# Centring the rows once, at the end of layer 2, and re-ordering ScalarE, VectorE and GpSimd around it

## The reference, cut to what matters

```
def _layernorm(x, axis=-1, eps=1e-05):
    m = jnp.mean(x, axis=axis, keepdims=True)
    v = jnp.var(x, axis=axis, keepdims=True)
    return (x - m) / jnp.sqrt(v + eps)
...
x = _layernorm(x + _L0_gnn_ref(x, adj, ...), axis=-1)   # attention, softmax over rows
x = _layernorm(x + _L1_gnn_ref(x, adj, ...), axis=-1)   # attention, softmax over columns, elu
x = _layernorm(x + _L2_gnn_ref(x, adj, ...), axis=-1)   # attention, softmax over rows, elu
x = _layernorm(x + _L3_gnn_ref(x, ..., adj, weight, bias), axis=-1)
# layer 3, with a 0/1 adjacency only relation 1 has edges:
#   y = (adj @ x) @ weight[0] + bias
```

## Time and profile before

| what | value |
|---|---|
| time, median of 3 runs | 412.65 us (412.54 to 412.78) |
| the profiled execution, its own time | 413.85 us |
| the profiled execution, its span (first to last instruction) | 411.7 us |
| busy share of the span: PE, PEld, DVE, ACT, POOL | 87%, 77%, 86%, 75%, 74% |
| TensorE clock granted, mean | 0.985 |
| 280 to 300 us (layer 2), busy of 20 us: PE, DVE, ACT, POOL | 19.45, 18.38, 15.24, 15.11 |
| 370 to 380 us (layer 3), busy of 10 us: PE, DVE, ACT, POOL | 9.86, 9.38, 8.23, 9.33 |
| 0 to 60 us | the only stretch in which the DMA engines are busy (0.84 and more of their time) |

### The profile page before, as it was taken

The page is one execution under the profiler, slowest core; times in us unless marked ns, Lnnn a source line. Parts: engine busy times, 40 slices in busy tenths (PEclk is TensorE's granted clock), DMA queues, the critical chain, the costliest instruction groups (busy, mean ns, idle before and its releaser), DMA issues. The chain is left out here.

```text
span 411.7 us, 9207 instructions
## 1 busy us (share of the span) xinstructions
PE 358.6 (87%) x2786; PEld 316.4 (77%) x2793; DVE 355.4 (86%) x1350; ACT 308.9 (75%) x840; POOL 304.9 (74%) x395
## 2 busy tenths in 40 slices
PE   7898999999977888887878889999999779999970
PEld 7697999999977877786878888989898665455550
DVE  0458899999999899999999987999899997899984
ACT  2757999999886776868878786878778647888862
POOL 5356889778788776886757757777777846999994
PEclk9999999999998999999999999999999999999995
DMA  6999973000000000000000000000000000022223
GB/s 164 219 249 247 264 113 53 2 1 2 2 1 2 1 2 0 2 2 0 2 1 2 2 0 2 3 0 2 2 1 2 2 1 0 2 78 78 76 77 108
DMA packets 8757, 18.20 MB, mean 44 GB/s; under 512 B 1281, under 2 KB 2561, under 8 KB 8705
## 3 DMA queue, kind: packets, MB, share of 16 engines
q0 software_dynamic: 2304, 8.39, 10.6%
q1 hardware_dynamic: 5280, 8.72, 6.3%
q10 hardware_dynamic: 1120, 0.46, 0.4%
HBM read 21.76 MB, written 4.19 MB: 63 GB/s over the span
## 5 line engine op out<-in xcount | busy, mean ns | idle before, releaser
L561 PE MATMUL o_ps<-h_scaled,PT 128*128 128x129 f32 (+1 forms) x1536 | 182.4, 277 | 10.3 <-POOL h_scaled L278 6.4
L561 PEld LDWEIGHTS o_ps<-h_scaled,PT 128*128 128x128 f32 x1536 | 176.7, 193 | 13.1 <-issue 9.6
L1043 DVE SCALAR_TENSOR_TENSOR PT<-rows_ps,factors,MT 128x512 f32<-128x512 f32 x128 | 88.7, 736 | 0.0
L805 ACT ACTIVATE X<-y,rstd 128x128 f32<-128x128 f32 x192 | 61.0, 390 | 25.0 <-POOL rstd L319 24.9
L319 POOL TENSOR_TENSOR rstd<-var_eps,neg_half 128x4 f32<-128x4 f32 x64 | 70.3, 1098 | 5.0
L498 PE MATMUL h_ps<-wx,xT 128*128 128x130 f32 x384 | 53.7, 283 | 14.0 <-DVE smax L1004 12.3
L498 PEld LDWEIGHTS h_ps<-wx,xT 128*128 128x128 f32 x384 | 48.5, 194 | 19.7 <-issue 19.5
L1119 DVE BATCH_NORM_STATS2 stats<-y 128x6 f32<-128x128 f32 x256 | 55.6, 280 | 5.8 <-DVE y L1113 0.9
L254 POOL TENSOR_TENSOR mean_term<-h_mean,empty_row 128x512 f32<-128x512 f32 x32 | 38.2, 1194 | 18.7 <-DVE residual L1099 14.1
L334 POOL TENSOR_TENSOR elu_exp<-elu_exp,X 128x512 f32<-128x512 f32 x32 | 40.8, 1275 | 6.7 <-ACT elu_exp L798 6.4
L278 POOL TENSOR_TENSOR h_scaled<-hx,factors 128x516 f32<-128x516 f32 x32 | 35.1, 1097 | 13.5 <-PE o_ps L561 8.2
(11 more groups left out here) (120 smaller groups left out, 660.0 us busy)
## 6 DMA issues: line engine op xcount, KB each, us to landing
MT<-adj_by_j POOLq DMA_DIRECT2D x16, 512.0 KB, 12.9
X<-x SPq DMA_DIRECT2D x16, 256.0 KB, 7.9
out<-X SPq DMA_DIRECT2D x16, 256.0 KB, 2.0
w_rel<-w SPq DMA_DIRECT2D x1, 256.0 KB, 3.5
w_back<-w_by_output ACTq DMA_DIRECT2D x1, 192.0 KB, 3.4
wx<-w_by_input ACTq DMA_DIRECT2D x1, 192.0 KB, 3.8
bias<-b ACTq DMA_DIRECT2D x1, 64.0 KB, 3.0
bias<-b SPq DMA_DIRECT2D x1, 64.0 KB, 5.5
```

Source lines behind the costliest of these rows:

```text
L561: last = pe.matmul(o_ps[it.b][:, ic, first:1 + D], PT[:, it.b, jc, ic * P:(ic + 1) * P], h_scaled[:, it.b, jc, first:1 + D], start=(jc == ...
L805: last = act.activation(X[:, it.g, c, :], y[:, it.b, c, :], ACT.Copy, scale=rstd[:, it.b, c:c + 1])
L1043: dve.scalar_tensor_tensor(out=PT[:, it.b, c, :], in0=rows_ps[:], scalar=factors[:, it.b, 1, c:c + 1], in1=m, op0=ALU.max, op1=ALU.mult, * ...
```

## The change

Rows now leave layer 2 centred. In layer 2 POOL runs `find_offset` and ACT `take_norm`; in layer 3 POOL no longer runs `find_offset`, and both ACT and DVE normalise by `y` times `rstd` alone. For that the first relation's weights and the layer's bias are centred over the output features by four small ACT operations in slots 38 to 41 (`CENTRE_LATE_SLOT` + 0 to 3), in place of PE's product and ACT's copy in slots 46 and 47. In layer 2 ACT copies `hx` and `xT` ahead of the normalisation; in layer 3 it normalises ahead of copying the sums. While item n+1 is of layer 2, DVE's `own_max` stands between the two pairs of `weights` instead of behind them.

```diff
--- before.py
+++ after.py
@@ -26,7 +26,7 @@
 
 LAST_ATTENTION, ATTENTION_END = G * LAYERS - 4, G * LAYERS + 3
 FLAG_SLOT = G * LAYERS + 6
-CENTRE_SLOT, CENTRE_LATE_SLOT = -3, G * LAYERS - 2
+CENTRE_SLOT, CENTRE_LATE_SLOT = -3, G * 2 + 6
 R_EIGHTY, EXPONENT, BIAS, Z, RZ, ABOVE, BELOW, HINGE, WEIGHT = range(9)
 LOWEST, BIG = -430.0, 3e38
 WARM_UP = 12
@@ -130,6 +130,9 @@
         rank_one = sb("rank_one", [P, P], BF16)
         bias2_col = sb("bias2_col", [P, 1])
         bias3 = sb("bias3", [P, D])
+        bias3_in = sb("bias3_in", [P, D])
+        late_scaled = sb("late_scaled", [P, D])
+        late_mean = sb("late_mean", [P, 2])
         ab2_sb = sb("ab2_sb", [P, 2])
         shift_k = sb("shift_k", [P, 5])
         b2_a = sb("b2_a", [P, 2])
@@ -202,7 +205,7 @@
                     sp.wait_ge(sem(f"mask_in{n - 4}"), 16)
                 load_x(item(n))
             sp.dma_start(w_rel[:, :, :], w3.rearrange("r d o -> d r o")).then_inc(sem("w_late"), 16)
-            sp.dma_start(bias3[:, :], b3.partition_broadcast(P)).then_inc(sem("w_late"), 16)
+            sp.dma_start(bias3_in[:, :], b3.partition_broadcast(P)).then_inc(sem("w_late"), 16)
 
             for n in range(G * LAYERS, G * (LAYERS + 1)):
                 it = item(n)
@@ -376,6 +379,8 @@
                     elu_low(at(-1))
                 if at(-2):
                     find_rstd(at(-2))
+                if at(-2) and at(-2).l == 2:
+                    find_offset(at(-2))
                 split_bias2(n)
                 if at(2) and at(2).l == 1:
                     column_weight(at(2))
@@ -388,13 +393,13 @@
 
                     pool.wait_ge(sem("y_sum"), it.done - 2)
                     pool.wait_ge(sem("x_new"), it.done - G)
+                    if it.g == 0:
+                        pool.wait_ge(sem("centred"), 3)
                     pool.tensor_tensor(residual[:, it.b, :, :], X[:, it.g, :, :],
                                        bias3[:, :].unsqueeze(1).broadcast_to([P, C, D]),
                                        ALU.add).then_inc(sem("residual"), 1)
                 if at(-1):
                     find_rstd(at(-1))
-                    if at(-1).g < FIRST_ON_VECTOR:
-                        find_offset(at(-1))
 
             def redo():
                 with pool.Fori(0, G) as g:
@@ -595,10 +600,6 @@
                     pe.wait_ge(sem("centre"), 1)
                     pe.matmul(rows_ps[:, 0:260], centre[:], wx[:, 1:3, :].rearrange("p l w -> p (l w)"),
                               start=True, stop=True).then_inc(sem("centred_ps"), 1)
-                if n == CENTRE_LATE_SLOT:
-                    pe.wait_ge(sem("hx"), G * LAYERS)
-                    pe.matmul(h_ps[:, 1, 0:D], centre[:], w_rel[:, 0, :], start=True, stop=True)\
-                        .then_inc(sem("centred_ps"), 1)
 
             def gather(it):
 
@@ -802,7 +803,7 @@
 
                 act.wait_ge(sem("rstd"), it.done)
                 for c in range(C):
-                    last = act.activation(X[:, it.g, c, :], y[:, it.b, c, :], ACT.Copy, scale=rstd[:, it.b, c:c + 1])
+                    last = act.activation(X[:, it.g, c, :], y[:, it.t, c, :], ACT.Copy, scale=rstd[:, it.t, c:c + 1])
                 last.then_inc(sem("x_new"), 1)
 
             def take_norm(it):
@@ -818,10 +819,16 @@
                     act.wait_ge(sem("centred_ps"), 1)
                     act.copy(wx[:, 1:3, :].rearrange("p l w -> p (l w)"), rows_ps[:, 0:260])\
                         .then_inc(sem("centred"), 1)
-                if n == CENTRE_LATE_SLOT + 1:
-                    act.wait_ge(sem("centred_ps"), 2)
-                    act.copy(w_rel[:, 0, :], h_ps[:, 1, 0:D])\
-                        .then_inc(sem("centred"), 1)
+                late = ((w_rel[:, 0, :], w_rel[:, 0, :]), (bias3_in[:, :], bias3[:, :]))
+                for k, (rows, to) in enumerate(late):
+                    if n == CENTRE_LATE_SLOT + 2 * k:
+                        act.wait_ge(sem("w_late"), 32)
+                        act.activation(late_scaled[:, :], rows, ACT.Copy, scale=-1.0 / D,
+                                       accum_out=late_mean[:, k:k + 1]).then_inc(sem("late_mean"), 1)
+                    if n == CENTRE_LATE_SLOT + 2 * k + 1:
+                        act.wait_ge(sem("late_mean"), k + 1)
+                        act.activation(to, rows, ACT.Identity, bias=late_mean[:, k:k + 1])\
+                            .then_inc(sem("centred"), 1)
 
             def flag(it):
 
@@ -861,19 +868,21 @@
                     node_factors(at(2))
                 if at(-1) and at(-1).l == 2:
                     elu(at(-1))
-                near_column_layer = any(at(k) and at(k).l == 1 for k in (1, -2))
-                if near_column_layer:
+                past_first_layer = any(at(k) and at(k).l >= 1 for k in (1, -2))
+                if past_first_layer:
                     take_next(at)
                 take_bias2(n)
                 if at(2) and at(2).l == 1:
                     above_max(at(2))
-                if at(-3) and at(-3).l != 1:
+                if at(-3) and at(-3).l == 0:
                     take_scaled(at(-3))
+                if at(-3) and at(-3).l == 2:
+                    take_norm(at(-3))
                 if at(-2) and at(-2).l == 1:
                     take_scaled(at(-2))
                 if at(1) and at(1).l == 1:
                     fill_empty(at(1))
-                if not near_column_layer:
+                if not past_first_layer:
                     take_next(at)
                 take_centred(n)
                 if at(2) and at(2).l == 1:
@@ -896,6 +905,8 @@
 
                         act.wait_ge(sem("sums"), it.of_layer - 4)
                     act.copy(split[:, it.r, 0, :, :], X[:, it.g, :, :]).then_inc(sem("split_hi"), 1)
+                if at(-3) and at(-3).g < FIRST_ON_VECTOR:
+                    take_scaled(at(-3))
                 if at(1):
                     it = at(1)
                     act.wait_ge(sem("sums"), it.of_layer)
@@ -903,8 +914,6 @@
 
                         act.wait_ge(sem("att"), it.done - 2)
                     act.copy(xT[:, it.b, :], sums_ps[it.b][:]).then_inc(sem("sum_taken"), 1)
-                if at(-3) and at(-3).g < FIRST_ON_VECTOR:
-                    take_norm(at(-3))
 
             def redo():
                 with act.Fori(0, G) as g:
@@ -1138,10 +1147,8 @@
             def normalize_last(it):
 
                 dve.wait_ge(sem("rstd"), it.done)
-                dve.wait_ge(sem("mean_var"), it.done)
                 for c in range(C):
-                    last = dve.tensor_scalar(X[:, it.g, c, :], y[:, it.t, c, :], mean_var[:, it.t, c, 0:1],
-                                             rstd[:, it.t, c:c + 1], ALU.subtract, ALU.mult)
+                    last = dve.tensor_scalar(X[:, it.g, c, :], y[:, it.t, c, :], rstd[:, it.t, c:c + 1], None, ALU.mult)
                 last.then_inc(sem("x_last"), 1)
 
             def attention_slot(at, n):
@@ -1169,9 +1176,12 @@
                     weights(at(1), (0, 1))
                 if at(-2) and at(-2).l != 1:
                     aggregate(at(-2))
+                early_max = at(1) and at(1).l == 2
+                if at(3) and early_max:
+                    own_max(at(3))
                 if at(1):
                     weights(at(1), (2, 3))
-                if at(3) and not (at(1) and at(1).l == 1):
+                if at(3) and not early_max and not (at(1) and at(1).l == 1):
                     own_max(at(3))
                 if at(3) and at(1) and at(1).l == 1:
                     take_max(at(3))
```

## The result

| | median | spread | runs |
|---|---|---|---|
| before, beside the change | 412.63 us | 412.54 to 412.78 | 4 |
| the change | 406.51 us | 405.24 to 407.46 | 4 |

The profiled execution of the change took 405.65 us for a span of 403.5, so against the profiled execution of before it gained 8.2 us.

What follows compares the result with a forecast made beforehand. It took a ring of two DVE/PE waits to bound layer 2 and POOL layer 3 and the end. Terms -2.8 + 0.5 + 1.1 - 2.05 - 1.9 = -5.15 us off 412.65 gave 407.5 us, 8-in-10 range 405.7 to 410.3.

Steps and rivals of the forecast that it cites:

- layer 2, own_max: Layer 2: early own_max removes DVE's wait for PE, period 6.54 to 6.26 us over ten items, -2.8 us.
- slots 32 and 33: Start of layer 2: DVE stands 1.4 us for hx, later idles take 0.9, leaving +0.5 us (bounds 0 and 1.4).
- ACT's operand, late operations, POOL's offset in layer 2: Layer 2: ACT's +0.37 us an item, four late operations and POOL's 0.49 us offset stay hidden, cost 0.
- hand-over: Slots 47 to 50: ACT's longer normalisations and wait for offset delay DVE's splits, +1.1 us (bounds 0.5 and 2.0).
- layer 3, ten items: Layer 3, steady: without POOL's offset PE paces at 3.48 us an item, -2.05 us over ten items.
- end, to the last normalisation: End: the last y starts 1.65 us sooner after PE's project_sum, plus 0.25 on item 62's normalisation, -1.9 us.
- behind the last normalisation: After the last normalisation: the output transfer stays, no gain.
- such a wait: Layer 2, every slot: own_max waits for hx, slower than before, 415.3 us at 0.5 an item; 6%.
- POOL's margin in layer 2: Layer 2: h_scaled still ends 0.12 us before DVE's y; if it overran, y would stand 0.3 us an item.
- POOL was to show gaps: Sign in layer 3: POOL, needing 3.27 us an item against PE's 3.48, would show gaps in the profile.
- POOL's backlog: End: the last y waited for ACT's normalisation, which waited for POOL's offset; the change leaves POOL no backlog.
- ACT's order: Layer 3: ACT's copy of the sums behind the normalisation, some 1.2 us later, needed only a gather later, cost 0.

Runs made afterwards that it cites:

- the last two experiments: Kernel before with layer 2's two re-orderings alone, 409.43 us; kernel before with ACT's layer 3 normalisation ahead of the sums' copy alone, 412.51 us.
- the other chip: The changed kernel timed once more with no edit, beside the kernel before: 405.58 us, ratio 0.9837.

## Why the prediction was right, and where it was not

| step | predicted | profiled execution | shown by |
|---|---|---|---|
| layers 0 and 1 | 0 | -1.3 | spread, not the change |
| layer 2, own_max | -2.8 | -2.9 | own_max late +2.85 by its trace, re-orderings alone -2.9 |
| slots 32 and 33 | +0.5 | +0.2 | 6.40 against 6.22 |
| ACT's operand, late operations, POOL's offset in layer 2 | 0 | 0 | 6.26 with and without them |
| hand-over | +1.1 | +0.8 | idles 1.46, 1.47, 0.82, 0.22 against 1.27, 1.11, 0, 0.67; 38.58 with ACT's normalisation behind the casts |
| layer 3, ten items | -2.05 | -1.9 | 34.92 in both kernels without offset |
| end, to the last normalisation | -1.9 | -2.1 | two causes, -1.1 and -1.0 |
| behind the last normalisation | 0 | -0.9 | 3.7 against 4.6 |

The rows add to -8.1, of a measured -8.2. How the hand-over's row comes about: take_max of slot 45 stands at 317.79, 4.1 us earlier than in the trace of before (321.90), and project_sum of item 52 at 357.25, 3.3 earlier. Timeline of DVE, the kernel before:

```profile
321.90 0.28 DVE L1004 TENSOR_REDUCE smax<-h_ps 128x1 f32<-128x128 f32 x1
...
341.49 0.69 DVE L1199 TENSOR_TENSOR split<-rest,split 128x512 bf16<-128x512 f32 x1 [1.27 <-ACT split L891]
...
347.45 0.71 DVE L1199 TENSOR_TENSOR split<-rest,split 128x512 bf16<-128x512 f32 x1 [1.11 <-ACT split L891]
```

**Layer 2.** The mechanism held in every part: PE's 6.26 is what is left, and the copy of hx ahead of the normalisation is what makes it possible. Without it the same own_max costs more than it gave. I had given such a wait 6%, and the experiment says how it looks: 0.33 us a slot. The stall in slots 32 and 33 was mis-sized: the wait itself came as worked out (1.33 us, "1.4"), but only 0.2 us of it were left behind DVE's later idles of 0.53 and 0.39, not 0.4 to 0.5; what took up the rest the rows don't show. The second wait, 0.64, cost nothing (248.59 - 242.35 = 6.24 us, with DVE's 0.38 of waiting for PE still in it).

**POOL's margin in layer 2.** I worked out 0.12 us between h_scaled and y. h_scaled ends at 256.25 and y starts at 256.36, 0.11 later, with its full 0.68; with the re-orderings alone, where this margin isn't used, the period is the same 6.26.

**The hand-over** came at +0.8 of +1.1, and by the cause I gave: with the normalisations behind the casts it takes 38.58 us, as in the kernel before (38.62). The place was one slot off: DVE's wait in slot 50, which I had grow from 0.67, shrank to 0.22, and one of 0.82 came in slot 49, where there had been none. Part of ACT's wait for the offset there is POOL's: `offset` took 0.46 us (345.40) instead of 0.20. What I did not see, and expected otherwise when I moved the normalisations (2.3 us), is that the waits which the kernel before has as well do not go with that edit: they come back as longer splits beside POOL's operations. Whether less or later work on POOL would get them back was not tried.

**Layer 3** went as worked out, but for one sign: POOL was to show gaps, and showed none between 357 and 392 us. var_eps and rstd keep their stretched 0.6 and 1.34 us while DVE works beside them. It did not matter, since 3.3 is under 3.48, but the margin is small: by these numbers 0.2 us more on POOL would reach 3.5 and pace again (an estimate). Tried was the offset's 0.49, which gives 3.76.

**The end.** The sum was right and its cause half wrong. I had ascribed it to POOL's backlog. Taking the offset out alone gives 9.70 - 8.58 = 1.1 us; the other 1.0 (8.58 - 7.62) comes from ACT's order, which I had costed at 0 because I looked only at whom the sums' copy makes wait (PE, a gather later) and not at whom the normalisation lets go (the buffer of y). Alone in the kernel before, that order gives nothing.

**Behind the last normalisation** I had put nothing. It is 4.6, 4.7 and 4.8 us from its end to the end of the span in the three kernels whose last two items end in one group of eight on DVE (before and the last two experiments), and 3.7 to 4.3 in the others, whose groups of four stand 1.26 to 1.55 us apart. One of the others is the kernel before without the offset (3.9), where nothing else of the output was touched. That the transfers stand closer together there is my reading; it was not tried by itself. Without these 0.9 us and the spread ahead of slot 32 the trace's gain is 5.9 us where 5.15 were forecast; the 0.75 between them are small misses that nearly all go one way, the stall of slots 32 and 33 (0.3) and the hand-over (0.3) above all. With the 0.9 it is 6.8, and the medians say 6.1 and, on the other chip, 6.9. So the 1.0 us between 407.5 and 406.51 has both parts in it.

## What to carry to other kernels

When an engine is freed of an operation, ask separately what paces the steady items and what frees the last buffers: here one edit on POOL moved the first, and the second needed ACT's order too. A wait that is removed from one engine's idle column can come back as a longer instruction on another; read the lengths of the operations behind it, not only the idles. And a re-ordering that brings a reader forward must bring its producer forward too, as far as the reader needs; here, without that, it turned into a loss in every slot (6.66 us against 6.54).

## What the runs showed of the hardware

- A DVE split (128x512, two SBUF inputs) that starts while POOL's residual or elu_exp (128x512) runs ends 0.54 to 0.56 us after it: 1.00, 1.19, 1.35 and 1.75 us long instead of 0.69. A start in the last 0.15 us of POOL's operation costs nothing (0.70 at 371.31 in the change).
- Beside POOL's `rstd` (128x4, 1.02 us) the same split isn't held up: 0.69 us at 343.91 in the change, begun 0.11 us into it.
- Small POOL operations are stretched beside DVE's split and `rest`: in the change var_eps takes 0.20 us alone and 0.56 to 0.76 in the middle of layer 3, rstd 1.02 and 1.34.
- Normalisation on DVE: with one operand from memory 0.84 to 0.88 us for four (L1151), with two 2.37 for eight (L1143).
- Normalisation on ACT: 1.28 us for four with one such operand, 1.64 or 1.65 with two, 0.09 each. The Trainium skill ("ScalarE: Activation LUTs", What ACT_TABLE_LOAD costs) gives about 93 ns for such an operand, and the rows agree.
